# Best-32 attention: VectorE marks a quarter of what lies below, and a shorter exact path

## The reference

```
scores = jnp.einsum('bthd,bghd->bhtg', Q, K) / np.sqrt(DH)
scores = jnp.where(vision_mask[:, None, None, :], scores, -jnp.inf)
topv, topi = jax.lax.top_k(scores, 32)
probs = jax.nn.softmax(topv, axis=-1)
attn = jnp.zeros_like(scores).at[bi, hi, ti, topi].set(probs)
attn_mean = attn.mean(axis=1)
c_t = jnp.einsum('btg,bgd->btd', attn_mean, x_vision @ Wv)
```

## Time and profile before

| what | value |
|---|---|
| median of 3 runs | 1140.82 us (1140.29 to 1145.69) |
| the profiled execution | 1140.79 us |
| its span, first to last instruction | 1139.5 us |
| TensorE matmuls, busy | 955.4 us (84%) |
| VectorE, busy | 848.7 us (74%) |
| ScalarE, busy | 651.4 us (57%) |
| GpSimd, busy | 295.7 us (26%) |
| mean granted TensorE clock | 0.892 of full |

### The profile page before, as it was taken

The page is one execution under the profiler, slowest core; times in us unless marked ns, Lnnn a source line. Parts: engine busy times, 40 slices in busy tenths (PEclk is TensorE's granted clock), DMA queues, the critical chain, the costliest instruction groups (busy, mean ns, idle before and its releaser), DMA issues. The chain is left out here.

```text
span 1139.5 us, 20829 instructions
## 1 busy us (share of the span) xinstructions
PE 955.4 (84%) x7631; PEld 599.1 (53%) x7648; DVE 848.7 (74%) x1772; ACT 651.4 (57%) x1067; POOL 295.7 (26%) x313
## 2 busy tenths in 40 slices
PE   5997859999999999996989989248878888987586
PEld 5876724444444444443668875134555556634354
DVE  5775789999899999942567876998878785265447
ACT  3442307788788888874445425059999997202121
POOL 1000088899600000000112521006373631000010
PEclk9999958999999999997789996567799989997797
DMA  5867642222222222200312228002363136830000
GB/s 178 310 234 272 239 134 61 76 79 83 76 74 79 81 79 77 74 1 12 103 49 77 71 61 221 1 1 60 97 181 87 56 98 209 203 110 1 1 1 19
DMA packets 99322, 111.83 MB, mean 98 GB/s; under 512 B 26658, under 2 KB 75731, under 8 KB 99219
## 3 DMA queue, kind: packets, MB, share of 16 engines
q1 hardware_dynamic: 96802, 109.50, 32.0%
q10 hardware_dynamic: 2416, 0.99, 0.4%
HBM read 80.95 MB, written 29.43 MB: 97 GB/s over the span
## 5 line engine op out<-in xcount | busy, mean ns | idle before, releaser
L835 ACT ACTIVATE pT<-bank 128x512 f32<-128x512 f32 x512 | 278.5, 597 | 93.2 <-PE bank L752 71.9
L857 DVE TENSOR_REDUCE rmax<-bank 128x2 f32<-128x1024 f32 x256 | 307.3, 1223 | 26.4 <-PE bank L720 25.4
L764 PE MATMUL bank<-pT,V 128*17 128x256 f32 x2048 | 161.1, 387 | 4.7 <-ACT oT L841 4.5
L1679 PE MATMUL bank<-K1s,qs 97*128 97x512 f32 x256 | 116.7, 558 | 54.7 <-ACT below L1788 36.7
L752 PEld LDWEIGHTS bank<-qs,ks 49*128 49x128 f32 x1024 | 77.7, 186 | 112.4 <-ACT pT L835 98.9
L1943 POOL TENSOR_TENSOR total<-total,work 128x1024 f32<-128x1024 f32 x40 | 94.8, 2378 | 159.0 <-ACT work L1797 158.1
L752 PE MATMUL bank<-qs,ks 49*128 49x256 f32 x1024 | 130.0, 332 | 2.3 <-ACT pT L835 0.5
L720 PE MATMUL bank<-ks,qs 49*128 49x512 f32 x512 | 110.6, 427 | 16.2 <-DMA ks<-k_parts_d 9.0
L1679 PEld LDWEIGHTS bank<-K1s,qs 97*128 97x128 f32 x256 | 54.8, 227 | 69.8 <-ACT below L1788 38.0
L1849 DVE MAX8 cand<-work 128x8 f32<-128x128 f32 x384 | 76.4, 278 | 0.0
L764 PEld LDWEIGHTS bank<-pT,V 128*17 128x17 f32 x2048 | 34.5, 95 | 63.2 <-ACT pT L835 44.7
(11 more groups left out here) (452 smaller groups left out, 1841.6 us busy)
## 6 DMA issues: line engine op xcount, KB each, us to landing
k_parts_d<-kparts SPq DMA_DIRECT2D x48, 512.0 KB
ks<-k_parts_d SPq DMA_DIRECT2D x381, 64.0 KB, 2.2
K1s<-k_parts_d SPq DMA_DIRECT2D x96, 128.0 KB
cn<-in_ctx SPq DMA_DIRECT2D x32, 384.0 KB, 4.0
cx<-in_ctx SPq DMA_DIRECT2D x16, 384.0 KB, 5.0
w<-in_L_ffn_w SPq DMA_DIRECT2D x32, 128.0 KB, 2.7
w2e<-in_L_ffn_w SPq DMA_DIRECT2D x16, 128.0 KB, 2.4
W<-in_L_xattn_W SPq DMA_DIRECT2D x2, 1024.0 KB, 8.3
```

The source lines that it names most:

```text
L764: t = pe.matmul(bank[32 * c:32 * c + VW, 7, a * S:(a + 1) * S], V[:, b * NCH + 4 * g + c, h, :], pT[:, (at + 2 * (c // 2) + a) % 8, c % 2 ...
L835: p_made.up(act.activation(pT[:, at % 8, :], bank[:, 4 + at % 3, :], ACT.Exp))
L857: max_read.up(dve.tensor_reduce(rmax[p % 2][:, :, qt, c], bank[:, b0:b0 + 2, :], AX.X, ALU.max))
L1679: m = pe.matmul(bank[:, b0 + c, :], qs1[0:NROW1, b * H1 + h, q], K1s[h][0:NROW1, keys], start=True, stop=(what == "new"))
```

## The change

The first of the four quarters of `below` is no longer marked by ScalarE but by VectorE, with ones: one instruction behind `settle`, which compares (score * scale) with the scaled threshold. TensorE subtracts these ones through a second `minus` matrix that holds -STEEP instead of -1. Scales now come from a tile `steep` [P, 2, 2], one pair for each of two tiles in flight; in the usual case `settle` copies the pair from `usual` ahead of the threshold. ScalarE marks one quarter (k = 1) and two quarters (k = 3) instead of two and two, and three single quarters in step 16.

In the exact case, the first eight best are taken from the candidates, so that the first search over 4096 scores goes; the final comparison goes too, since scales of 1 and -1 with a threshold of 1e30 make marks out of the replaced scores directly. Three memsets of one column stand in place of one.

```
-    minus = sb("minus", [P, P], BF16)
+    minus = sb("minus", [P, 2, P], BF16)
+    steep, usual = sb("steep", [P, 2, 2]), sb("usual", [P, 2])
...
-                pe.wait_ge(*below_made.at(4 * t + k + 1))
+                pe.wait_ge(*(below_made.at(3 * t + k) if k else marked.at(t + 1)))
...
-                    m = pe.matmul(bank[:, b0 + c, :], minus[:, :], below[:, keys], start=False, stop=True)
+                    m = pe.matmul(bank[:, b0 + c, :], minus[:, k == 0, :], below[:, keys], start=False, stop=True)
...
-                                         scale=-STEEP), n)
+                                         scale=steep[:, t % 2, 0:1]), n)
...
                     if k % 2:
-                        mark_below(s - 1, k - 1, 2)
+                        mark_below(s - 1, k // 2 + 1, k // 2 + 1)
...
                 if s == NTL:
-                    mark_below(s - 1, k, 1)
+                    if k:
+                        mark_below(s - 1, k, 1)
                     if k == 0:
+                        act.wait_ge(*picked.at(s))
                         sum_best(s - 1)
...
             with dve.If_ne(flagged, 0):
-                for k in range(KTOP // 8):
+                exact.up(dve.match_replace(home(t)[:, :], top[j][:, 0:8], home(t)[:, :], LOW))
+                for k in range(1, KTOP // 8):
                     take8(top[j][:, 8 * k:8 * k + 8], home(t)[:, :], home(t)[:, :], exact)
-                dve.wait_ge(*exact.at(NEX * t + 8))
-                exact.up(dve.tensor_scalar(home(t)[:, :], home(t)[:, :], LOW, -1e18, ALU.not_equal, ALU.mult))
-                exact.up(dve.memset(steep_thr[:, j:j + 1], 0.0))
+                exact.up(dve.memset(steep[:, j, 0:1], 1.0))
+                exact.up(dve.memset(steep[:, j, 1:2], -1.0))
+                exact.up(dve.memset(steep_thr[:, j:j + 1], FAR))
             with dve.If_eq(flagged, 0):
+                dve.tensor_copy(steep[:, j, :], usual[:, :])
                 dve.tensor_scalar(steep_thr[:, j:j + 1], top[j][:, KTOP - 1:KTOP], STEEP, None, ALU.mult).then_inc(exact.sem, NEX)
...
+        def mark_first(t):
+            if t:
+                dve.wait_ge(*s_made.at(nth["cut", t - 1, 0] + 1))
+            marked.up(dve.tensor_scalar(below[:, 0:1024], home(t)[:, 0:1024], steep[:, t % 2, 1:2],
+                                        steep_thr[:, t % 2:t % 2 + 1], ALU.mult, ALU.is_lt))
...
-        minus_made.up(dve.tensor_scalar(minus[:, :], identb[:, :], -1.0, None, ALU.mult))
+        for k, by in enumerate((-1.0, -STEEP)):
+            minus_made.up(dve.tensor_scalar(minus[:, k, :], identb[:, :], by, None, ALU.mult))
+            vec.do(dve.memset(usual[:, k:k + 1], (2 * k - 1) * STEEP))
...
                     settle(s - 1)
+                    mark_first(s - 1)
```

More of the change, by code:

```diff
@@ L1532, in build @@
     NCN = 4
-    LOW = -3e38
+    LOW, FAR = -3e38, 1e30
     STEEP = 2.0 ** 66
     below = sb("below", [P, S2], BF16)
-    minus = sb("minus", [P, P], BF16)
+    minus = sb("minus", [P, 2, P], BF16)
     cand = sb("cand", [P, NG, 8])
@@ L1560, in build @@
         "s_made", "s_taken", "sel", "over_made", "over_summed", "over_in", "exact", "picked"))
-    lsum_made, ebias_made, added, below_made, e_summed = (flag(n) for n in (
-        "lsum_made", "ebias_made", "added", "below_made", "e_summed"))
+    lsum_made, ebias_made, added, below_made, marked, e_summed = (flag(n) for n in (
+        "lsum_made", "ebias_made", "added", "below_made", "marked", "e_summed"))
     late_added = flag("late_added")
@@ L1724, in best_tensor @@
             piece("new", 0, k)
-        pe.wait_ge(*minus_made.at(1))
+        pe.wait_ge(*minus_made.at(2))
         for g in range(4 * (NTL + 1)):
@@ L1880, in settle @@
             if t >= 2:
-                dve.wait_ge(*below_made.at(4 * (t - 1)))
+                dve.wait_ge(*below_made.at(3 * (t - 1)))
             dve.reg_load(flagged, over_i[j][0:1, 0:1])
             with dve.If_ne(flagged, 0):
-                for k in range(KTOP // 8):
+                exact.up(dve.match_replace(home(t)[:, :], top[j][:, 0:8], home(t)[:, :], LOW))
+                for k in range(1, KTOP // 8):
                     take8(top[j][:, 8 * k:8 * k + 8], home(t)[:, :], home(t)[:, :], exact)
-                dve.wait_ge(*exact.at(NEX * t + 8))
-                exact.up(dve.tensor_scalar(home(t)[:, :], home(t)[:, :], LOW, -1e18, ALU.not_equal, ALU.mult))
-                exact.up(dve.memset(steep_thr[:, j:j + 1], 0.0))
+                exact.up(dve.memset(steep[:, j, 0:1], 1.0))
+                exact.up(dve.memset(steep[:, j, 1:2], -1.0))
+                exact.up(dve.memset(steep_thr[:, j:j + 1], FAR))
             with dve.If_eq(flagged, 0):
+                dve.tensor_copy(steep[:, j, :], usual[:, :])
                 dve.tensor_scalar(steep_thr[:, j:j + 1], top[j][:, KTOP - 1:KTOP], STEEP, None, ALU.mult).then_inc(exact.sem, NEX)
```

## The result

In 20 runs each on the same chip the changed kernel took 1145.83 us (1139.34 to 1154.12) and the kernel before 1140.77 us: a ratio of 1.0039, 95% interval 1.0021 to 1.0056. That is 5.1 us more, within half a per cent, as forecast; the forecast was 2.8 us more. The profiled execution took 1148.67 us (span 1147.0). A gain and a loss of several microseconds each stand behind the small difference.

The account below looks back on a forecast made before the run. ScalarE and VectorE were taken to bound the loop, VectorE's search chain the exact path. From 1140.8 us, -6.7 for the exact path and +9.5 for the steps gave 1143.6 us; range 1132 to 1147.5.

Parts of the forecast that it names:

- What bounds the loop: Steps 2 to 16: ScalarE and VectorE both bound within a microsecond; VectorE's step grows by 0.76 us, to 12.8 when short.
- its chain "of about 4.9 us": Longer steps: TensorE, at 1.2 GHz for part, bounds them from the turned quad to the next subtraction, about 4.9 us.
- The exact path, -6.7: Tile 0's exact search: first search -4.49 us, comparison -2.29, two more memsets +0.1, all on the chain.
- The copy is held, `mark_first` is not: Ten steps with adds: the copy waits for GpSimd's running add, some 2 us; `mark_first` then runs free at 0.80 us.
- Marking at x + 5.2: Step 8, x being GpSimd's first add's start: ScalarE marks at x + 5.2 instead of x + 3.09, 2.1 us late.
- The size of the loop's loss: Steps 2 to 16: 4.2 + 4.4 - 0.4 + 2.0 - 0.7 = +9.5 us, end included.
- ScalarE's 0.85: Steps 2 to 15: ScalarE's first marking shrinks from 2048 to 1024 elements, saving 0.85 us a step.
- rival 4: Loop: both instructions held in some steps, or TensorE at 1.2 GHz in more; 4 to 6 us more, 1148; chance 0.13.
- ScalarE's scale: ScalarE's markings: reading the scale from a tile costs between nothing and 0.1 us each, left out of the sum.
- Rival 1: Loop: GpSimd's adds hold neither the copy nor `mark_first`; 1131.7 us; chance 0.13.
- Rival 2: Loop: only `mark_first` is held, the small copy is not; about +1.8 us for the loop, 1135.2 us; chance 0.17.

Follow-up runs that it names:

- both cures: The changed kernel with one-column memsets replacing the two-element copy, and GpSimd's first add of a step waiting for `mark_first`: 1136.5 us beside 1142.51, ratio 0.9948.
- copy-alone kernel: The kernel before plus only the two-element copy from `usual` to `steep` ahead of the threshold, its result unread: 1162.7 us beside 1142.73, ratio 1.0177.

## Why the prediction was right

By its own steps, with what each measured:

1. **What bounds the loop.** "Both engines bound this loop within a microsecond": right for the short steps and the fast long ones. Free of the hold, VectorE waits for nobody in the short steps, at 12.81 to 12.82 us (forecast 12.8). In the other long steps TensorE is a third bound, as the forecast has it; its chain "of about 4.9 us" stands in no row, and no run tested it.
2. **The exact path, -6.7.** Measured -6.2. The search, the comparison and the memsets are as in the sum; the miss is the idle behind the branch, 1.31 us ahead of the first replacement where it was 0.73 ahead of the first search. The forecast allowed for it but put nothing in. This idle is not a price of the missing search: it was 0.73 us in both profiles of the kernel that lacks only the search, and between 0.77 and 1.39 us in those with the changed exact path. With 0.77, in the kernel with both cures, cast to `ntop` took 32.60 us, which is the 6.7 us to the digit.
3. **The copy is held, `mark_first` is not.** Right in kind, and shown: take away either the width of the copy or the add beside it and the cost goes. I had only a 32x17 copy that was held and a one-column scaling that was not the earlier trace rows; two elements go with the former. The Trainium skill (SBUF — State Buffer, "Who interferes with whom") says that an instruction in a two-port mode and one of GpSimd exclude each other for the whole instruction, whoever issued first going first; this trace agrees where GpSimd was first, with the copy of step 8 ending 0.03 us behind GpSimd's add. None of GpSimd's adds here was seen held by VectorE. The ten copies that meet adds took 1.21 to 2.31 us, 1.77 on average, the other five 0.17. `mark_first` was not held because the copy ahead of it was, as the forecast says; with memsets in the copy's place it took up to 2.31 us instead of 0.80.
4. **Marking at x + 5.2.** x + 5.09 in step 8; in step 4, where the add began at 784.55, x + 5.00 (789.55).
5. **The size of the loop's loss.** +9.5 forecast, +11.0 measured (11.6 less 0.6 at the end). Long steps with adds: 14.40 to 14.44 us in four of the six (forecast 14.4), but the step into 9 took 15.05 and the one into 13 15.99, which the forecast had at 14.4; in sum +6.2, forecast +4.2. The step into 13 alone is 1.6 us over, the largest single miss. Short steps +5.4 for three (forecast +5.2), and ScalarE's 0.85 did not come back behind them (the step into 6 took 12.81 against 12.45, a miss of 1.2), for by then VectorE, not ScalarE, was last. Step 15 went the other way: +1.0 up to its `ntop`, forecast +2.0; step 16 gave back 0.65 up to its `ntop` and 0.6 up to the last marking, 1.25 in all, forecast 0.7. The steps into 10 and 14 give -0.9 and +0.2, forecast -0.4 and 0. So +11.0 lies near +9.5 partly because misses of both signs cancel.
6. **The step from 12 to 13.** Here is a piece of rival 4. The windows of the changed kernel (length, busy us of PE, PEld, DVE, ACT, POOL, then the granted clock, DMA share and GB/s):

```profile
888.00:902.00 14.00, 11.45 (x55) 7.46 (x56) 12.91 (x53) 12.23 (x16) 9.55 (x4) 1.00 0.23 64
902.00:910.00 8.00, 5.94 (x20) 4.41 (x18) 7.65 (x32) 7.88 (x11) 4.75 (x2) 0.67 0.12 38
```

   TensorE waited for ScalarE's late work (it stood 1.87 us ahead of 904.81) and was granted 0.67 of full in that stretch, so for much of it 1.2 GHz. Its subtraction of the last quarters came later, ScalarE stood 1.59 us ahead of 911.83, the one-column sum was 0.92 us late for VectorE's cast, and the copy then found the next add fresh and was held for 2.31 us. That the idle caused the fall is argued from their order; no run tested it.
7. **ScalarE's scale.** "Between nothing and 0.1 us each, left out": it is 0.09. This case's trace agrees with the Trainium skill (ScalarE: Activation LUTs, "What ACT_TABLE_LOAD costs"), where each operand read from a tile adds about 93 ns. It should have been in the sum: of the 0.85 us that ScalarE saves in a step, two times 0.09 go again. Most of it was covered here because VectorE was last.

Rival 1 is the kernel without a hold: two versions of it took 7.1 and 6.0 us less than before, not 9.1; one reason is that the fast long steps did not get down to 12.4 but to 12.8 at best. Rival 2 is what the memsets make: 4.0 us less, 5.6 forecast. So the hold costs the changed kernel 11 to 12 us, and the forecast's own difference between its case and rival 1 was 11.9.

## What to carry to other kernels

An instruction's length in isolation is not its price: ahead of a chain that another engine waits for, look at what GpSimd runs at that moment, and keep copies of two columns or more, and wide scalings, out of it. Two columns are cheaper written by two one-column instructions; better still is to put GpSimd's work behind VectorE's short chain where GpSimd has idle time, which heals everything in the chain at once. And where two engines bound a loop within a microsecond, moving work from one to the other may only move the wait; here no gain from the move could be told.

## What was not expected of the hardware

- A copy of 128x2 in fp32 takes 0.17 us alone and up to 2.33 us beside GpSimd's add; two copies of 128x1 beside the same adds take 0.14 to 0.16 us each.
- The hold ends with the add: two adds ran back to back (840.00 to 844.78), and the copy that came in the second was let in only behind it. A copy that comes in the first of two is let in between them: 784.44 to 784.87 in the copy-alone kernel, with adds to 784.85 and from 784.80. No held instruction took longer than one add (2.33 us at most for the copy, an add being 2.38), and the adds were not lengthened by what they held (4.67 to 4.80 us for two, as before).
- 15 such copies cost a whole kernel 20 us, 1.8%, more than their own 16.1 us of busy time. Six of them, held for 1.95 to 2.33 us each, are 13.5 of the 16.1.
